# Local attention's projection behind the transpositions, and a quarter of the scan's multiply by C on GpSimd

## The reference

```python
def step(h, inputs):
    u_t, d_t, b_t, c_t = inputs
    dA = jnp.exp(d_t[..., None] * A)
    h = dA * h + (d_t * u_t)[..., None] * b_t[:, None, :]
    y = jnp.einsum('bdn,bn->bd', h, c_t)
    return (h, y)
```

```python
h = shift_token(x)
q, k, v = jnp.split(h @ wqkv, 3, axis=-1)        # then heads, l2norm, scales, rotary
sim = jnp.einsum('bhwid,bhwjd->bhwij', bq, bk)
sim = jnp.where(mask, -jnp.finfo(sim.dtype).max, sim)
attn = jax.nn.softmax(sim, axis=-1)
out = jnp.einsum('bhwij,bhwjd->bhwid', attn, bv)
x = x + o @ wo
```

## Time and profile before

| | us |
|---|---|
| median of 3 runs | 3891.34 |
| lowest and highest | 3886.89 and 3895.9 |
| the profiled execution | 3895.95 |
| its span | 3893.4 |
| granted clock of TensorE, mean | 0.911 of full speed |

### The profile page before, as it was taken

The page is one execution under the profiler, slowest core; times in us unless marked ns, Lnnn a source line. Parts: engine busy times, 40 slices in busy tenths (PEclk is TensorE's granted clock), DMA queues, the critical chain, the costliest instruction groups (busy, mean ns, idle before and its releaser), DMA issues. The chain is left out here.

```text
span 3893.4 us, 65456 instructions
## 1 busy us (share of the span) xinstructions
PE 2985.4 (77%) x22063; PEld 1733.9 (45%) x22143; DVE 2724.8 (70%) x4138; ACT 1552.9 (40%) x2219; POOL 1742.9 (45%) x1111
## 2 busy tenths in 40 slices
PE   3677465659988994999889983667666599879987
PEld 1112354523434442666556662223222366646765
DVE  4699546447766763887478855698699688648874
ACT  3532123124444553555245532432433255425542
POOL 4465121131111102886078813465366488428861
PEclk8699678669999997999999996899899799989999
DMA  3354000032111200111011100242143111101110
GB/s 83 91 147 111 7 6 7 1 92 39 34 32 28 39 15 22 35 36 33 1 31 37 37 6 4 99 146 102 65 147 135 29 37 38 22 7 39 37 29 22
DMA packets 141586, 187.95 MB, mean 48 GB/s; under 512 B 74218, under 2 KB 88641, under 8 KB 141121
## 3 DMA queue, kind: packets, MB, share of 16 engines
q1 hardware_dynamic: 141388, 185.41, 18.0%
HBM read 132.76 MB, written 9.18 MB: 36 GB/s over the span
## 5 line engine op out<-in xcount | busy, mean ns | idle before, releaser
L249 POOL TENSOR_TENSOR arena<-arena 128x1024 f32<-128x1024 f32 x192 | 451.2, 2351 | 232.9 <-DVE arena L258 178.2
L1425 DVE TENSOR_REDUCE causal_peak_parts<-psum 128x1 f32<-128x512 f32 (+3 forms) x608 | 385.3, 661 | 142.1 <-PE psum L1300 77.1
L1904 POOL TENSOR_TENSOR arena<-arena,w_minus_half 128x16 f32<-128x16 f32 x128 | 372.8, 2912 | 175.8 <-DVE arena L1836 175.8
L1408 ACT ACTIVATE arena<-psum 128x1024 f32<-128x1024 f32 (+3 forms) x352 | 294.3, 870 | 342.4 <-PE psum L1331 165.7
L233 ACT ACTIVATE psum<-arena,w_A 128x1024 f32<-128x1024 f32 x192 | 214.4, 1118 | 460.7 <-DVE arena L258 387.8
L258 DVE TENSOR_TENSOR_SCAN arena<-psum,arena 128x1024 f32<-128x1024 f32 x160 | 364.5, 2279 | 28.5 <-POOL arena L249 28.5
L1902 POOL TENSOR_TENSOR arena<-arena 128x1024 f32<-128x1024 f32 x128 | 301.9, 2359 | 103.4 <-DVE arena L1830 103.4
L207 PE MATMUL psum<-arena,m_sel 96*128 96x512 bf16 x384 | 117.7, 389 | 229.4 <-DVE arena L273 202.1
L1640 PE MATMUL psum<-w_layer_wqkv,arena 128*128 128x512 f32 x512 | 266.1, 646 | 33.9 <-DVE arena L1830 32.5
L1775 ACT ACTIVATE arena<-arena 128x1024 f32<-128x1024 f32 x128 | 135.3, 1057 | 375.1 <-DVE arena L1851 375.1
L1297 PE MATMUL psum<-arena 128*128 128x512 bf16 (+3 forms) x746 | 229.3, 347 | 45.0 <-PEq L1033 25.1
(11 more groups left out here) (338 smaller groups left out, 6594.8 us busy)
## 6 DMA issues: line engine op xcount, KB each, us to landing
arena<-scan_rows_large SPq DMA_DIRECT2D x128, 512.0 KB, 3.7
arena<-arena SPq DMA_DIRECT2D x256, 130.0 KB, 2.3
arena<-scan_rows_small SPq DMA_DIRECT2D x128, 256.0 KB, 3.8
arena<-causal_parts SPq DMA_DIRECT2D x288, 64.0 KB
causal_parts<-arena SPq DMA_DIRECT2D x8, 768.0 KB, 3.8
arena<-Z SPq DMA_DIRECT2D x128, 32.0 KB, 1.8
arena<-Z SPq DMA_DIRECT2D x128, 28.0 KB, 1.8
X<-in_L_attn_a_x SPq DMA_DIRECT2D x4, 512.0 KB, 6.2
```

The source lines that it names most:

```text
L249: pool.tensor_tensor(inputs[:, s % 2], b_lane[:, s % U], du(*runs[o]), ALU.mult).then_inc(input_up.sem, 1)
L1408: act.activation(into, place, ACT.Exp, scale=SCALE).then_inc(probs.sem, 1)
L1425: dve.tensor_reduce(part[:, heads[0]:heads[0] + len(heads), qt, half:half + 1].rearrange("p h a -> p (h a)"), place[:, 0:len(heads) * size ...
L1904: pool.tensor_tensor(RN[:, s4, :], SS[:, s4, :], k.minus_half[:, 0:2 * HEADS], ALU.pow).then_inc(rn_in.sem, 1)
```

## The change

**Scan.** The multiply by C is split by columns. VectorE does tokens 0 to 767 (`MAIN`), GpSimd 768 to 1023. GpSimd can't read PSUM, so ScalarE copies these 256 columns of C from bank 3 into a new SBUF tensor `c_rest` of two slots (`keep_c`). VectorE's multiply waits for that copy in place of TensorE's spread of C. TensorE's fold waits for both parts. GpSimd's product (L249) now runs two steps ahead in its own order: product i+2, then the rest of multiply i.

**Local attention.** TensorE's order in a step changes: `output(i-2)` moves from behind `values` to behind `turn_qk`; `turn_in(i+4)` moves from behind `masks` to ahead of `turn_probs`; `masks(i+1)` moves to the end of the step. ScalarE copies the input (`copy_h`) ahead of `copy_probs`. VectorE adds tile i-3 in place of i-2, and two adds more than before stand at the end of a pass. SyncE's order is unchanged.

```diff
@@ scan
+            def keep_c(o, j, s):
+                act.wait_ge(c_up.sem, c_up.at(o * J + j + 1))
+                act.wait_ge(weighted_rest.sem, weighted_rest.at(o * J + j - 1))
+                act.copy(c_rest[:, s % 2], two(2)[:, MAIN:SEQ]).then_inc(c_kept.sem, 1)
...
+            def weigh_rest(o, j, s):
+                i = o * J + j
+                pool.wait_ge(scanned.sem, scanned.at(i + 1))
+                pool.wait_ge(c_kept.sem, c_kept.at(i + 1))
+                pool.wait_ge(summed.sem, summed.at(i - 1))
+                pool.tensor_tensor(weight[:, s % 2, MAIN:SEQ], state[s % U][:, MAIN:SEQ], c_rest[:, s % 2], ALU.mult).then_inc(
+                    weighted_rest.sem, 1)
...
-                dve.wait_ge(c_up.sem, c_up.at(i + 1))
+                dve.wait_ge(c_kept.sem, c_kept.at(i + 1))
                 dve.wait_ge(summed.sem, summed.at(i - 1))
-                dve.tensor_tensor(weight[:, s % 2], state[s % U], two(2), ALU.mult).then_inc(weighted.sem, 1)
+                dve.tensor_tensor(weight[:, s % 2, 0:MAIN], state[s % U][:, 0:MAIN], two(2)[:, 0:MAIN], ALU.mult).then_inc(
+                    weighted.sem, 1)
@@ local_attention, TensorE
                 if before:
                     values(i - 1, 1 - s)
-                if before > 1:
-                    output(i - 2, i + 4 if ahead > 3 else TILES)
                 if ahead > 2:
                     project_qk(i + 3, (s4 + 3) % RING)
                 if ahead:
                     project_v(i + 1, (s4 + 1) % RING)
+                if ahead > 3:
+                    turn_in(i + 4, s4, i - 2 if before > 2 else 0)
                 turn_probs(i, s)
                 if ahead:
                     turn_qk(i + 1, (s4 + 1) % RING)
-                    masks(i + 1)
-                if ahead > 3:
-                    turn_in(i + 4, s4, i - 1 if before > 1 else 0)
+                if before > 1:
+                    output(i - 2, i + 5 if ahead > 3 else TILES)
                 if before:
                     turn_out(i - 1, ahead)
+                if ahead:
+                    masks(i + 1)
```

More of the change, by code:

```diff
@@ L153, in scan @@
     lane_in = [k.count(f"scan_lane_in{s}") for s in range(U)]
-    credited = (input_up, scanned, weighted, summed, y_taken)
+    c_kept, weighted_rest = k.count("scan_c_kept"), k.count("scan_weighted_rest")
+    credited = (input_up, scanned, weighted, weighted_rest, c_kept, summed, y_taken)
+    MAIN = 3 * SEQ // 4
     for s in credited:
@@ L162, in scan @@
         state = [ring2[:, 1, 0], ring2[:, 1, 1]] + spare
+        c_rest = mem.enter_context(nc.sbuf_tensor(k.name("scan_c_rest"), [P, 2, SEQ - MAIN], F32))
         bank = k.bank
@@ L219, in body @@
                     spread_c(*ahead(o, j, 1))
+                pe.wait_ge(weighted_rest.sem, weighted_rest.at(o * J + j + 1))
                 for c in range(2):
@@ L237, in body @@
                     decay_of(*ahead(o, j, 2), s)
+                keep_c(o, j, s)
             for j in range(2):
@@ L244, in _, with product @@
         def _(pool):
-            def body(o, j, s):
+            def weigh_rest(o, j, s):
[5 more added lines that the diff above has]
+                    weighted_rest.sem, 1)
+            def product(o, j, s):
                 i = o * J + j
@@ L249, in body @@
                 pool.tensor_tensor(inputs[:, s % 2], b_lane[:, s % U], du(*runs[o]), ALU.mult).then_inc(input_up.sem, 1)
+            def body(o, j, s):
+                if ahead(o, j, 2):
+                    product(*ahead(o, j, 2), s + 2)
+                weigh_rest(o, j, s)
+            for j in range(2):
+                product(0, j, j)
             steps(pool, body)
@@ L279, in scan @@
     n = len(runs)
-    for s in (c_up, decay_up, input_up, scanned, weighted, summed):
+    for s in (c_up, decay_up, input_up, scanned, weighted, weighted_rest, c_kept, summed):
         s.passed(n * J)
@@ L1799, in step @@
                     square(i + 3, 1 - s)
+                if ahead > 3:
+                    copy_h(i + 4, s4)
                 copy_probs(i)
@@ L1805, in step @@
                     copy_out(i - 1)
-                if ahead > 3:
-                    copy_h(i + 4, s4)
             in_steps(act, step, lambda i, s4: copy_out(i))
@@ L1880, in step @@
                     normal(i - 1, 1 - s)
-                if before > 1:
-                    add(i - 2)
+                if before > 2:
+                    add(i - 3)
                 if ahead > 1:
@@ L1893, in finish @@
                 normal(i, s4 % 2)
+                add(i - 2)
                 add(i - 1)
```

## The result

The changed kernel takes **3909.6 us** (median of 20 runs, 3899.6 to 3918.3). The kernel before takes 3892.1 beside it (20 runs, 3881.3 to 3905.2). The ratio is 1.0045, 95% interval 1.0035 to 1.0054: slower by 17.5 us. The time lies inside the range of 3870 to 3925 and just outside the forecast's own 3873 to 3906. The likeliest outcome was forecast as within 0.2% of before; it is 0.45% slower.

A forecast was written before the change was run, and what follows sets the result against it. VectorE was taken to bound the scan, TensorE first and VectorE second the local attention. The scan's -48 and the local +46 summed to -2, giving 3889 us for the median, range 3870 to 3925.

The forecast's parts named there:

- The scan: Scan step: VectorE's multiply shrinks to 768 columns, the step from 3.31 to 3.06 us, 48 us gained over 192 steps.
- the margin of 0.12: Scan: GpSimd's step was put at 2.94 us, under VectorE's 3.06 by 0.12.
- rival 1: Scan: GpSimd binds, so the scan gains only 0 to 25 us; time 3912 to 3937; chance 0.20.
- The circle: Local attention: take_v releases SyncE's fetch, turn_in waits for it, the next take_v follows; tile 9.07 to 9.40, 36 us lost.
- the local term of the sum: Local attention: 36 us for the circle, 5 for entering it, 5 for the last three tiles; +46 us.
- add moved from tile i-2 to i-3 costs nothing, one more at the end.: Local attention: VectorE's add one tile later was priced at nothing, including the extra add at a pass's end.
- the 5 that the prediction had for the projection in the last three tiles: Ends of local passes: the projection stands behind the softmax instead of beside it, 0.4 x 3 x 4 = 5 us.
- 36 + 5: Local attention: 36 us lost to the circle over 27 turns x 4 passes, plus 5 for entering it once per pass.
- (2) The circle doesn't bind: Local attention: SyncE issues or lands earlier than read; 8.85 us per tile, -24 us, time 3819; chance 0.12.
- (3) A longer circle: Local attention: slow issues throughout or slowest landing, 2.4 us; up to 0.7 x 108 = 76 more, 3965; chance 0.05.
- (4) The two engines block each other: Scan: GpSimd and VectorE block each other, GpSimd's step 4.26 us, +182 us, time 4119; chance 0.03.

The follow-up runs named there:

- the third experiment: The changed kernel with add(i-2) moved ahead of the last normal at the end of a local pass: 3903.4 us, ratio 1.0031.
- the one with 704 columns: The scan's part alone on the kernel before, with VectorE taking 704 columns and GpSimd 320: 3840.5 us.
- the two controls: The kernel before with SyncE's fetch issued one step earlier, 3886.0 us; the kernel before with five fetch DMAs in place of four, 3883.4 us.
- the fastest: The changed kernel with the add put back, SyncE's fetch one step earlier and masks ahead of turn_out: 3799.1 us, ratio 0.9756.
- the three others with the new order: Local part alone on the kernel before, 3965.5 us; changed kernel with turn_in and copy_h behind the projection, 3833.0; changed kernel with five fetch DMAs, 3988.4.

## Why the prediction came out as it did

**The scan was right.** -48 was forecast and -49.5 measured, -46.8 by itself. The multiply takes 0.925 us (0.94 forecast), the copy 0.373 (0.39), the product 2.35 as before. GpSimd's small multiply takes 0.731, not 0.69, so the margin of 0.12 came out as 0.05. It held, and rival 1 stood 64 columns away.

**The circle was right**, with its place, its partners and its size. The links, from the rows above: `take_v` ends at 1711.83, first DMA 0.09 later, 3.88 to the fourth, landing and `turn_in` by 1717.51, 0.16 to `turn_probs`, 1.08 to `copy_probs`, 2.27 to the end of `take_v`. In the mean of the 108 turns they are 0.10, 4.10, 1.74, 0.16, 1.09 and 2.27: 9.46, the sum that the prediction had. From scores to scores a tile of a loop's middle takes 9.16 to 9.42 and one at its edge 9.71 to 9.88; a loop's first turns take up to 10.7. The mean of tiles 12 to 28 is 9.37 to 9.41.

**What failed was the local term of the sum, +46 where +65 was measured (52.1 + 12.8).** Two steps of it:

1. *"add moved from tile i-2 to i-3 costs nothing, one more at the end."* This is the larger miss. The ends of the passes were put at nothing and cost 12.8 us. The moved step was followed through the loop, and the finish was settled in half a sentence. There the add stands behind the last `normal`, and TensorE's next projection waits for it: 1.16 us a pass, 4.6 in all, as the third experiment shows by putting it back. Another 0.4 a pass remains then (11.17 against 10.77). It is the projection that now stands in the last step's chain, ahead of `turn_out`: ScalarE's copy of what `turn_out` writes starts at 1838.83, behind a wait, and `values` needs that bank read, so that `values` starts 3.14 after `turn_probs` (1839.51 - 1836.37) where it was 2.72. These 1.6 us belong to the 5 that the prediction had for the projection in the last three tiles; with the 2.1 inside the passes that term came to 3.7. The remaining 6.6 is the granted clock, of which the prediction said nothing. Why it falls stays open.
2. *"Sum 9.46, made of one tile's rows to within some 0.1; I take 9.40."* The rounding went the wrong way: 0.06 x 108 = 6 us. And the tile before was taken as 9.07, where the 27 turns of a pass had 9.04 each (243.9 to 244.2): 3 us more. So the circle and entering it cost 49.5 us and not 36 + 5. The slow issues in a loop's first turns don't explain it: they are in the 4.10 of the prediction, and the queue of the kernel before has them too (up to 5.5 from the first DMA to the sixth), hidden there.

With 9.46 against 9.04 and 1.16 a pass for the add, the sum would have been -48 + 45 + 5 + 5 + 5 = +12, 0.3% slower: the right side, though still short by what the clock takes. That the time lies inside the stated range says little for the sum: the local miss of 19 us fits into it.

**The rivals.** (1) GpSimd binds: no, by nothing to spare; at 320 columns it does. (2) The circle doesn't bind: no, but its price was right: with the circle broken the tile is 8.84 (8.85 forecast) and the kernel takes 3826 (3819 forecast). (3) A longer circle: not here, but made by hand, 0.6 us longer, it costs 79 us; the prediction had up to 76 for 0.7. (4) The two engines block each other: no.

The Trainium skill ("Perfetto Trace Analysis", section "Optimizing Scalar/DVE Operations") warns that the two share an SBUF read port, so that moving work between them might not help. Here it helped: both of VectorE's operations in a step have one operand in PSUM, the products stay at 2.353 us, and moving a quarter of the multiply gained 47 us. Whether the operand in PSUM is the reason was not tried. The Trainium skill's fixed cost of about 2.0 us ("DMA: Bandwidth & Descriptors", section "Anatomy of one DMA") is given there for DMAs that GpSimd issues, and these are SyncE's, so it should not have been set against them. The trace decides: this transfer lands in 1.7 us, and in nearly every turn `turn_in` starts 1.7 to 1.8 after the fourth issue, which leaves no room for 0.3 more.

## What to carry to other kernels

An operation moved earlier in one engine's order brings its input's deadline with it: follow that input back through the queue that issues it, and add up the whole circle. If it closes above the pace of the loop, the idle time only changes its name; a fetch issued one step earlier (and one add put back) turned +17 us into -68 here.

Every moved step has an end of the loop, too. The order that the finish leaves, who waits for it, and what idles there deserve the same sum as the middle, times the number of passes.

## What the hardware did that was not expected

**The granted clock at the ends of the passes.** It stayed at 1.00 in all four ends of the kernel before, 10.76 to 10.77 us each, and in the 16 ends of the four other kernels with the old local order (the scan's part alone, the one with 704 columns, the two controls), 10.76 to 10.78. In the new order it fell in 22 of 28, and how far differs from pass to pass of one kernel: 0.72, 0.88, 1.00, 0.88 in the changed one; 0.87, 0.87, 1.00, 0.75 with the add put back; 0.86 and three times 1.00 with the early fetch; four times 0.86 or 0.87 in the fastest; in the three others with the new order it fell in 11 of 12. The ends of the fastest as stretches, the first:

```profile
1805.28:1818.10 12.82, 9.62 (x78) 8.28 (x78) 2.73 (x8) 3.24 (x4) 0.00 (x0) 0.87 0.01 1
```

A fall costs 1.3 to 5.5 us (17.86 at 0.57 in the local part alone, against 12.33 at 1.00). What all 28 ends share is TensorE's idle time before the last `turn_probs`, 2.61 us where the kernel before has 1.52, since the projection no longer stands in that place; the six in which the clock stayed have it too. Idle time in the loop is not needed for it, for the fastest kernel has none. Whether the 2.61 us is the cause was not tried, and why one pass escapes and the next doesn't stays open.

**SyncE's issue is the scarce thing, not the transfer.** The DMA that `take_v` releases, its neighbour and three of a fetch hold the fourth back by 3.9 us, and by up to 5.3 in a loop's first turns, against 1.7 for the landing. A fifth adds 0.6 to every tile where the queue is in the circle, and nothing where it isn't.
